# Mixture-of-experts blocks that gather their rows by row number instead of reading scattered copies, with the first block written out ahead of the loop

## What is computed

```python
x = x + tanh(g_xattn) * ((1 - gamma) * layernorm(x) + gamma * A_learned)
xt = layernorm(x)
probs = softmax(xt @ gate_w.T)
expert_weights, expert_indices = top_k(probs, 2)      # then divided by their sum
x1 = silu(einsum('ti,eoi->teo', xt, w1))
x3 = einsum('ti,eoi->teo', xt, w3)
y = einsum('teo,eio->tei', x1 * x3, w2)
out = x + tanh(g_ffn) * sum over the 2 chosen experts of weight * y
```

## Time and profile before

| | |
|---|---|
| median of 3 executions | 831.4 us (825.93 to 832.64) |
| the profiled execution | 832.5 us |
| its span, first to last instruction | 830.9 us |
| TensorE (PE) busy | 739.2 us, 89% of the span |
| VectorE (DVE) busy | 396.6 us |
| ScalarE (ACT) busy | 287.0 us |
| GpSimd (POOL) busy | 148.0 us |
| granted TensorE clock, mean | 0.92 of full speed |

### The profile page before, as it was taken

One profiled execution on the slowest core, in us unless ns is written; L12 is line 12 of the kernel. 1 busy time (PEld: TensorE's weight loads), 2 busy tenths in 40 slices (PEclk: granted clock), 3 DMA queues, 4 the chain that ended last, 5 costly groups with the idle time before them and its releaser, 6 DMA issues.

```text
span 830.9 us, 11032 instructions
## 1 busy us (share of the span) xinstructions
PE 739.2 (89%) x3434; PEld 598.1 (72%) x3435; DVE 396.6 (48%) x930; ACT 287.0 (35%) x475; POOL 148.0 (18%) x199
## 2 busy tenths in 40 slices
PE   7393079835999999999999999999999999999996
PEld 3193058734888888888888888888888888888885
DVE  3988964763228222652246328322662282265222
ACT  4744536523117112621135117111541261153111
POOL 1371001774101110011101000110010110101010
PEclk9755577758999999999999999999999999999999
DMA  8742031643821821164213621821155118211111
GB/s 303 316 161 101 20 133 52 256 180 129 329 38 25 328 38 38 38 219 135 49 27 110 245 51 25 302 65 38 25 172 207 25 28 326 51 26 38 25 28 23
DMA packets 23727, 98.18 MB, mean 118 GB/s; under 512 B 2784, under 2 KB 3040, under 8 KB 19872
## 3 DMA queue, kind: packets, MB, share of 16 engines
q0 software_dynamic: 10992, 66.21, 25.4%
q1 hardware_dynamic: 12576, 31.81, 11.1%
q10 hardware_dynamic: 144, 0.00, 0.0%
HBM read 73.72 MB, written 24.30 MB: 118 GB/s over the span
## 4 chain that ended last, share of the span: by engine, by line
issue 71%; DVE 9%; POOL 8%; PE 6%; POOLq 3%; DVEq 1%; DMA 1%; ACT 0%; SPq 0%
POOL out L434 4%; POOL routed L399 3%; DVE front L853 2%; PE bank L501 2%; PE bank L503 2%; PE bank L514 1%; POOLq L255 1%; PE bank L466 1%; POOLq L433 1%; DVE top L951 1%; DVE ln_stats L811 1%; DVE front L948 1%; DVE rows_own L828 1%; POOL raw L442 1%; PE bank L456 1%
## 5 line engine op out<-in xcount | busy, mean ns | idle before, releaser
L547 PE MATMUL bank<-w_hi,xT_hi 128*128 128x512 f32 x560 | 225.3, 402 | 2.1 <-DVE xT_lo L1117 2.1
L548 PE MATMUL bank<-w_hi,xT_lo 128*128 128x512 f32 x560 | 222.0, 396 | 0.0
L549 PE MATMUL bank<-w_lo,xT_hi 128*128 128x512 f32 x560 | 221.5, 396 | 0.0
L755 ACT ACTIVATE act_g<-bank 128x512 f32<-128x512 f32 x70 | 41.7, 596 | 327.6 <-PE bank L549 327.6
L547 PEld LDWEIGHTS bank<-w_hi,xT_hi 128*128 128x128 f32 x560 | 105.6, 189 | 26.3 <-issue 2.5
L549 PEld LDWEIGHTS bank<-w_lo,xT_hi 128*128 128x128 f32 x560 | 105.4, 188 | 25.8
L548 PEld LDWEIGHTS bank<-w_hi,xT_lo 128*128 128x128 f32 x560 | 105.7, 189 | 23.5
L547 PE MATMUL bank<-w_hi,hT_hi 128*128 128x512 f32 x280 | 115.9, 414 | 0.0
L1011 DVE TENSOR_TENSOR w_lo<-raw,w_hi 128x1024 fp32r<-128x1024 f32 x88 | 104.2, 1220 | 20.0 <-ACT w_hi L671 18.3
L1133 DVE TENSOR_TENSOR hT_lo<-bank,hT_hi 128x512 fp32r<-128x512 f32 x70 | 48.4, 692 | 136.8 <-ACT hT_hi L759 136.8
L671 ACT ACTIVATE w_hi<-raw 128x1024 fp32r<-128x1024 f32 x88 | 91.4, 1060 | 59.2 <-PE bank L549 50.4
(11 more groups left out here) (190 smaller groups left out, 687.4 us busy)
## 6 DMA issues: line engine op xcount, KB each, us to landing
raw<-weights POOLq DMA_DIRECT2D x21, 2048.0 KB, 15.3
xtile<-routed SPq DMA_DIRECT2D x36, 260.5 KB, 2.6
raw<-weights SPq DMA_DIRECT2D x3, 2048.0 KB, 7.4
xb<-x SPq DMA_DIRECT2D x4, 1024.0 KB, 11.8
raw<-xT SPq DMA_DIRECT2D x4, 1024.0 KB, 9.0
w_hi<-weights POOLq DMA_DIRECT2D x2, 2048.0 KB, 10.0
out<-xb SPq DMA_DIRECT2D x4, 1024.0 KB, 4.3
routed<-pad SPq DMA_DIRECT2D x8, 260.5 KB, 2.2
```

Source lines behind the costliest of these rows:

```text
L547: nc.tensor.matmul(out_ap, hi, hi_w, start=start, stop=False)
L548: nc.tensor.matmul(out_ap, lo, hi_w, start=False, stop=False)
L549: return nc.tensor.matmul(out_ap, hi, lo_w, start=False, stop=stop)
L755: nc.scalar.activation(act_g[:, s, :], bank[GATE[s]][:, :], ACT.Silu).then_inc(silu_set[s], 1)
```

## The change

No row is scattered any more. SyncE stores x1 of each batch to the DRAM tensor `found`, with a small tail for each token (8 expert weights, token number, scale and shift of the layer norm; ROW is now 523). For each block there is a list of 128 row numbers. It comes from products of one-hot matrices: VectorE writes for each of the 16 picks of a tile pair which slot of a block the pick has (`slots`), GpSimd writes which block it has, times the token's two digits (`columns_of`, 32 tensor_scalars of 128x136 for each pair), and TensorE multiplies the two (`all_blocks`). Routing is done for two batches at a time. VectorE turns the products into row numbers (`order_blocks`, which reads seven table entries). **Block 0** is gathered from the first two batches alone and its matmuls stand ahead of the loop, mixed with the routing of the second pair; the loop starts at block 1. Each block's rows now come by an indirect DMA on GpSimd's queue (`gather`), and ScalarE normalises them in place (`normal_x`) after `silu(0)`.

```diff
-            def route(b, tiles):
...
-                        nc.gpsimd.indirect_dma_start(
-                            routed, bass.IndirectOffsetOnAxis(ap=place_i[:, b, i, k:k + 1], axis=0),
-                            rows[b][:, i, :], None, bounds_check=E * REGION - 1, oob_is_err=True,
-                        ).then_inc(routed_in[b], 16)
+            def columns_of(q):
...
+                for m in range(PICKS):
...
+                    nc.gpsimd.tensor_scalar(in_column[:, m, 0, :], columns[:, :], column[:, i, k:k + 1], part_no[:, :], ALU.is_equal, ALU.mult)
+                    last = nc.gpsimd.tensor_scalar(in_column[:, m, 1, :], columns[:, :], column[:, i, k:k + 1], tile_no[:, t:t + 1],
+                                                   ALU.is_equal, ALU.mult)
+            def gather(at):
+                nc.gpsimd.indirect_dma_start(
+                    xtile[:, :], None, found, bass.IndirectOffsetOnAxis(ap=at, axis=0),
+                    bounds_check=P + TOKENS - 1, oob_is_err=True,
+                ).then_inc(xtile_in, 16)
...
+            def add_y(g):
+                pool.wait_ge(y_set, g + 1)
+                nc.gpsimd.tensor_tensor(y_row[:, :], token_out[:, :], no_shift[:, :], ALU.add)
+                pool.drain()
...
+            def next_x(g):
+                pool.wait_ge(xtile_free, g + 1)
+                nc.gpsimd.tensor_tensor(x_row[:, :], rows_now[:, :], no_shift[:, :], ALU.add)
+                pool.drain()
+                gather(x_row[:, 0:1])
+
+            def next_weights(e):
                 for q in range(GROUPS):
                     pool.wait_ge(lo_set[q], OPS * e + OPS)
                     pool.dma_start(raw[:, q, :], w_groups[bass.ds(e + 1, 1), q, :, :].squeeze(0)).then_inc(raw_in[q], 16)
+
+            def add_blocks(e):
+                with blocks(pool, e) as g:
+                    next_x(g)
+                    add_y(g)
...
+            next_x(0)
+            next_weights(0)
+            add_y(0)
+            pool.wait_ge(table_set, 1)
+            add_blocks(0)
+            with pool.Fori(1, E - 1) as e:
+                next_weights(e)
                 add_blocks(e)
             add_blocks(E - 1)
...
+            def normal_x(n):
+
+                act.wait_ge(xtile_in, n * 16)
+                nc.scalar.activation(xtile[:, 0:D], xtile[:, 0:D], ACT.Identity, bias=xtile[:, SHIFT:SHIFT + 1],
+                                     scale=xtile[:, SCALE:SCALE + 1]).then_inc(xn_set, 1)
...
                     with act.Else():
                         silu(0, nth)
+                        normal_x(nth + 1)
                         silu(1, nth)
                         h_high(0, nth)
                         x_high(nth + 1)
...
-            def transpose_x(n):
-                pe.wait_ge(xtile_in, n * 16)
+            def transpose_x(n, into=X_BANK):
+                pe.wait_ge(xn_set, n)
...
+            first_low(1, range(2, OPS))
+            V.memset(small[:, 5:6], 0.0).then_inc(y_out, 1)
+            choose(1)
+            leads(1)
+            places(1)
+            product(0, 1, OPS)
+            slots(1)
+            split_low(2, 0, [0])
+            h_low(0, 1)
+            product(1, 1, OPS)
+            weights_of(1)
+            split_low(2, 0, [1])
+            h_low(1, 1)
+            second_rows()
+            split_low(2, 0, range(2, OPS))
+            tabulate()
+            order_blocks()
+            scale_y(0, 0, OPS)
+            x_low(2, X_EARLY[1])
+            next_rows(2).then_inc(xtile_free, 1)
+            take_meta()
```

More of the change, by code:

```diff
@@ L39 @@
 EPS = 1e-5
-SOON = 2
 E, I = 8, 1024
@@ L331, in _ @@
+            store_x1(2)
+            store_x1(3)
+            store_meta(1)
         @block.gpsimd
@@ new lines, in early_blocks, with all_blocks @@
+            def early_blocks():
+                pe.wait_ge(early_hot_set, 1)
+                for i in range(PAIR):
+                    last = nc.tensor.matmul(early_row_ps, early_hot[:, i, :], row_parts[:, i, :], start=(i == 0), stop=(i == PAIR - 1))
+                last.then_inc(early_row_mm, 1)
+            def all_blocks(q):
+                pe.wait_ge(slot_set, q + 1)
+                pe.wait_ge(column_set, q + 1)
+                for m in range(PICKS):
+                    last = nc.tensor.matmul(rows_ps, in_slot[:, m, :], in_column[:, m, :, :], start=(q == 0 and m == 0),
+                                            stop=(q == 1 and m == PICKS - 1))
+                last.then_inc(rows_mm, 1)
@@ L683, in even_rows @@
                     act.wait_ge(x1_set, 2 * TB)
-                for i in range(TB):
+                for i in tiles:
                     act.wait_ge(AA_mm, TB * b + i + 1)
@@ L759, in h_high @@
                 nc.scalar.activation(hT_hi[:, s, :], bank[H_BANK[s]][:, :], ACT.Copy).then_inc(hhi_set[s], 1)
-            x_high(1)
-            for b in (1, 2):
-                act.wait_ge(routed_in[b], 16 * 2 * TB)
-            act.wait_ge(raw_in_0[2], 16)
-            split_high(2, range(OPS))
+            silu(0, 1)
+            silu(1, 1)
+            h_high(0, 1)
+            h_high(1, 1)
+            normal_x(2)
+            x_high(2, X_EARLY[1])
             act.wait_ge(table_set, 1)
@@ L1058, in choose, with slots, weights_of @@
+            def slots(q):
+                dve.wait_ge(early_row_mm, 1)
+                if q > 0:
+                    dve.wait_ge(rows_mm, q)
+                dve.drain()
+                for m in range(PICKS):
+                    last = V.tensor_scalar(in_slot[:, m, :], from_one[:, 0:P], slot[:, m // 2, m % 2:m % 2 + 1], None, ALU.is_equal)
+                last.then_inc(slot_set, 1)
+            def weights_of(q):
+                dve.wait_ge(share_set, q + 1)
                 V.tensor_scalar(share[:, :, :], share[:, :, :], tanh_f, None, ALU.mult)
```

574 lines of the change are left out of this document (340 added, 234 removed).

## The result

The changed kernel takes 1113.1 us (median of 4 runs, 1108.8 to 1118.1), the kernel before, measured beside it, 828.9 us (median of 4): 1.344 times as long, 95% interval 1.339 to 1.350. The profiled execution took 1110.4 us, its span is 1108.8. I had forecast 1057 us and a range up to 1100: the direction was right, the size was 56 us short.

The account below looks back on a forecast made before the run. PE was taken as the bound, never waiting from 211.31 us on, 18.0 us a block. Front -3.7, block 1 +8.4, first blocks +136, ordinary +45 and last +40 gave +226 us: 1057 us, range 980 to 1100.

Parts of the forecast that it names:

- The drain: On GpSimd, ahead of each gather: a drain ends only when GpSimd's DMAs have landed, so x now waits.
- Rival 1: The drain waits only behind large loads; ordinary blocks cost 0, last ones 19 us; 988 us in all; chance 0.22.
- First blocks: First block of experts 1 to 6: gather held behind 6 MB of weights, 22.7 us each, 136 us in all.
- ordinary blocks: 20 blocks of the loop: gather waits for the accumulating DMA to land, 2.25 us each, 45 us in all.
- rival 2: A gather takes 4.8 us like the accumulating DMA, and the clock falls in last blocks: 1121 us; chance 0.12.
- T+26.8: Mean time after a block's start on PE (T) when the gather behind weights starts, over six first blocks.
- Block 1: The loop's first block: its gather is late behind weights, +6.5 us and 1.9 for the clock, +8.4 us.
- Last blocks: Last block of seven experts: ScalarE's weight splits come after the late normalisation, 5.7 us each, 40 us in all.
- The front: Everything before block 1: it starts at 207.6 instead of 211.3, -3.7 us, bounds -12 and +6.
- Rival 3: Not slower: the stall belongs to the accumulating DMA, so gathers behind weights land in time; 828 us; chance 0.06.
- rival 4: More blocks than 35, through padding of expert 0; one more would be 18 us, 1075 us; chance 0.02.

Follow-up runs that it names:

- run 1: Changed kernel with the gather reading row numbers where VectorE wrote them, without the copy's drain; queue order kept: 1018.2 us, ratio 1.226.
- run 8: Changed kernel plus 32 comparisons and scalings of several widths on GpSimd alone after its last wait, to price them: 1151.8 us (one run).
- run 4: Changed kernel with the 64 column comparisons issued by VectorE instead of GpSimd: 1082.4 us, ratio 1.302.
- run 11: Run 9 with block 2's gather also ahead of block 0's accumulation and the first weights held until it landed: 821.6 us, ratio 0.990.
- run 3: Changed kernel with the loop's gather put ahead of the block's accumulation; queue, drain and weights stay: 896.9 us, ratio 1.077.
- run 6: Changed kernel with gather ahead of accumulation, columns on VectorE and weights from SyncE's queue: 828.5 us, ratio 1.000.
- run 10: Changed kernel without the drain before the gather and with weights from SyncE; accumulation still first, columns on GpSimd: 942.9 us, ratio 1.139.
- run 2: Changed kernel with the next expert's weights issued from SyncE's queue; the drain stays: 1021.7 us, ratio 1.230.
- run 9: Run 6 with the table of rows split around block 1's columns and first weights held until block 1's gather landed: 828.2 us, ratio 1.001.

## Why the prediction was right and wrong

**The drain** (right, and half the story). "A drain of GpSimd ends when its DMAs have landed" is shown by the waits of 19.07 and 3.85 us, and by run 1, in which ordinary blocks fell to 17.7 us once the drain was gone. Rival 1, no wait behind small DMAs, is refuted by the 3.85 us. But its other half, the queue's order, is true: run 1 shows that it would have held the first blocks at 36 us without any drain. Here theory and rival were not alternatives; the time was nearly the same by either in first blocks, so the forecast could hardly go wrong there. The gather of run 1, issued right behind the weights, landed 17.9 us after its issue. The Trainium skill (DMA: Bandwidth & Descriptors, SWDGE vs HWDGE vs iDMA) says that within one queue of one DMA engine descriptors start in order; the trace agrees.

**First blocks** (136 forecast, 134 measured) and **ordinary blocks** (45, 49): right. The gather landed in 3.5 us by the median, for which I had taken 3.3; rival 2 needed 4.8. Behind weights it left at T+25.5, the mean of the six places, where I had T+26.8.

**Block 1** (8.4, 9.5, of which 2.1 are the front's): right. **Last blocks** (40, 49): right in mechanism, 1.3 us short each, since what I had kept for the upper bound, that the clock falls in each, is what happened. PE's timeline of one has the wait, and behind it four transposes of h in 1.05 us (0.60 at full clock in the earlier trace rows, there of the next rows); it is the same in all seven:

```profile
312.19 0.79 PE L598 MATMUL bank<-w_hi,hT_hi 128*128 128x512 f32 x1 [4.42 <-DVE hT_lo L1304]
...
313.63 1.05 PE L620 MATMUL bank<-ident,h 128*128 128x128 f32 x4
```

**The front** is the step that failed, in one term, the price of GpSimd's comparisons: "10 us from 175 ... between 0.18 and 0.77 us each ... and I take 0.3, being nearer to the small one". A set of 32 took 32.6 us (152.88 to 185.5) and 28.4 us (195.41 to 223.8); one takes 0.81 us alone, where I had 0.3. Two things were wrong in it. I chose by width, between a copy of one element and a scaling of 512, and took the end that looked nearer; run 8 shows that the operation decides as much, a comparison costing four times a scaling's price per element. For the same reason the upper end, 0.77, was no bound: it came from another operation.

The term also cost something in my sum only once, on the second set. At 0.3 us each the first set, begun at 152.9, would have ended near 163, ahead of the 167 at which I had PE start block 0. It ended at 185.5: PE waited 18.5 us for it and started block 0 at 188.9. It also held what stood behind it on GpSimd, the scales of batches 2 and 3, until 188.8, and with them the choice of experts' shares and the second columns, for which PE waited another 23.1 us. DVE's timeline shows the hold:

```profile
188.84 0.26 DVE L1153 SCALAR_TENSOR_TENSOR lead<-gap,meta 128x8 f32<-128x8 f32 x2 [16.37 <-POOL meta L407]
```

With the columns off GpSimd (run 4) block 1 starts at 213.3; my 207.6 was then 5.7 us early, within the bounds I gave the front. So of the 39 us of error in the front 33.3 are this term and what it held; the other 5.7 lie within what I had allowed for a chain laid out by hand, and no run takes them apart.

**Rival 2's** 1121 us lies nearest to the measured time, but by luck: its larger part, a gather of 4.8 us in all 34 blocks, is not what happened, and only its smaller one, the clock in the last blocks, came true. **Rival 3**, not slower, fell with the waits above, **rival 4** with the 35 blocks.

**The version that comes out 1% ahead.** What is left once the waits are gone is small. By the yardstick of y's scaling, in one execution of each, the front of run 11 is 5.8 us shorter than before's (205.9 against 211.7) and the 34 pitches 4.1 us (607.9 against 612.0), an ordinary one taking 17.7 us instead of 18.0; why it does stays open. Everything else that the runs took back was cost of placement: gather behind accumulation (runs 3, 11), weights in the gather's queue (runs 6, 10), comparisons on GpSimd (run 4).

## What to carry to other kernels

A transfer that GpSimd issued was held here in three ways: by the drain (19.07 us behind weights), by the queue's order (17.9) and by what flew beside it (9.7 from issue to landing instead of 3.5). Lift one and the next shows, so order the queue by who waits, urgent reads first. Price an instruction that the trace doesn't have by its operation as well as by its size, and take no bound from another operation. And count what stands behind a slow instruction on its engine, not only the one who reads its result.

## What the runs showed that I had not expected

- GpSimd's comparison costs 3.3 ns per element of a row against 0.83 for multiply and add (run 8); at 136 wide the same instructions started 0.225 us apart on VectorE and 0.80 apart on GpSimd.
- Beside VectorE's work single ones of these took up to 2.69 us on GpSimd. The longest of them fell beside two splits on VectorE, and all of those from 172.65 to 185.5, while VectorE stood idle, took 0.81. No run shows the cause by an edit. Timelines of DVE and POOL in the changed kernel:

```profile
162.38 2.36 DVE L1124 TENSOR_TENSOR w_lo<-raw,w_hi 128x1024 fp32r<-128x1024 f32 x2
...
162.65 2.69 POOL L418 TENSOR_SCALAR scratch<-columns,column,part_no 128x136 bf16<-128x136 bf16 x1
165.33 0.81 POOL L419 TENSOR_SCALAR scratch<-columns,column,tile_no 128x136 bf16<-128x136 bf16 x1
```

- GpSimd's drain leaves another engine's DMAs out (run 2), but feels them: behind one accumulation it took 7.22 us beside two of SyncE's 2 MB loads (run 2) and 10.71 beside three (run 9), 3.85 us without.
